# A graph-attention layer and a 32-expert feed-forward on one core: how tokens reach their experts and how the sums come back

## The reference, cut to what matters

```python
N, D, E = 3125, 256, 100000           # nodes, width, edges; 32 experts of hidden width 64
x1 = layernorm(x)
q, k, v = x1 @ wq + bq, x1 @ wk + bk, x1 @ wv + bv
scores = sum(q[dst] * k[src]) * D**-0.5 + edge_weight * we + be
attn = segment_softmax(scores, dst)
y = layer_norm(x1 + segment_sum(v[src] * attn, dst) + x1 @ ws + bs, g1, b1)
y = layer_norm(y + gelu(y @ w_ff1 + b_ff1) @ w_ff2 + b_ff2, g2, b2)
x = x + y
f = layernorm(x)
e = argmax(f @ router_w.T + router_b)   # one expert for each token
h = relu(f @ W1[e] + b1[e])             # W1[e]: 256 x 64
out = x + relu(h @ W2[e] + b2[e])       # W2[e]: 64 x 256
```

## Time and profile before

| | us |
|---|---|
| median of 3 runs | 1901.17 |
| lowest and highest run | 1875.29, 1903.03 |
| span of the profiled execution | 1885.6 |
| PE, DVE, ACT, POOL busy in the span | 1656.9, 1193.9, 965.5, 300.8 |

### The profile page before, as it was taken

One profiled execution on the slowest core, in us unless ns is written; L12 is line 12 of the kernel. 1 busy time (PEld: TensorE's weight loads), 2 busy tenths in 40 slices (PEclk: granted clock), 3 DMA queues, 4 the chain that ended last, 5 costly groups with the idle time before them and its releaser, 6 DMA issues.

```text
span 1885.6 us, 41069 instructions
## 1 busy us (share of the span) xinstructions
PE 1656.9 (88%) x11015; PEld 1378.6 (73%) x11015; DVE 1193.9 (63%) x3327; ACT 965.5 (51%) x2962; POOL 300.8 (16%) x397
## 2 busy tenths in 40 slices
PE   2898999999799999999899999999999789419960
PEld 1796888888688888887688888888888779315640
DVE  3927898988688889898555555555555578701111
ACT  1566888888588888887233333333333345103210
POOL 0022000000000000000111111111110067375435
PEclk9999999999899999999999999999999889656555
DMA  6054333333433333334822222222210100047634
GB/s 159 28 129 115 104 105 104 106 103 105 140 104 104 106 105 103 104 105 112 164 76 77 76 76 76 76 78 75 76 75 37 53 17 0 6 117 214 181 113 121
DMA packets 226999, 180.40 MB, mean 96 GB/s; under 512 B 41884, under 2 KB 218038, under 8 KB 223544
## 3 DMA queue, kind: packets, MB, share of 16 engines
q1 hardware_dynamic: 189327, 112.46, 21.6%
q0 software_dynamic: 21408, 61.20, 9.7%
q10 hardware_dynamic: 16224, 6.27, 1.5%
HBM read 84.94 MB, written 99.11 MB: 98 GB/s over the span
## 4 chain that ended last, share of the span: by engine, by line
PE 78%; DVE 6%; DMA 5%; POOL 4%; issue 3%; SPq 2%; ACT 1%; POOLq 0%; DVEq 0%; ACTq 0%
PE bank L1371 29%; PE bank L1404 15%; PE bank L1392 11%; PE bank L1356 9%; PE bank L1411 3%; PE bank L1486 3%; PE bank L1493 2%; PE bank L1478 2%; PE bank L1444 2%; PE bank L1436 2%; POOL arena L691 2%; POOL xs_dram L669 2%; SPq L458 1%; DMA V<-in_x 1%; DMA arena<-in_x 1%
## 5 line engine op out<-in xcount | busy, mean ns | idle before, releaser
L784 ACT ACTIVATE arena<-bank,tables 128x128 f32<-128x128 f32 x2048 | 585.2, 369 | 144.5 <-PE bank L1356 144.4
L1371 PE MATMUL bank<-arena 128*125 128x128 f32 x4096 | 585.9, 286 | 11.8 <-DVE arena L1055 11.8
L1371 PEld LDWEIGHTS bank<-arena 128*125 128x125 f32 x4096 | 488.4, 188 | 65.1 <-DVE arena L1055 11.9
L1055 DVE TENSOR_TENSOR arena<-iota_row,tables 128x250 f32<-128x250 f32 x1024 | 421.1, 412 | 0.1
L1081 DVE SCALAR_TENSOR_TENSOR arena<-arena,tables,bank 125x128 f32<-125x128 f32 x1023 | 351.9, 344 | 86.5 <-PE bank L1371 37.1
L1404 PE MATMUL bank<-V,arena 125*125 125x256 f32 x1250 | 296.4, 382 | 5.6 <-ACT arena L810 5.6
L810 ACT COPY arena<-bank 125x500 f32<-125x500 f32 (+1 forms) x175 | 90.8, 533 | 379.5 <-PE bank L1411 379.5
L1404 PEld LDWEIGHTS bank<-V,arena 125*125 125x125 f32 x1250 | 223.3, 188 | 38.0 <-ACT arena L810 10.3
L1122 DVE CUSTOM_DVE_ANT_0 arena<-arena 125x3200 f32<-125x3200 f32 x25 | 87.3, 3493 | 222.2 <-ACT arena L793 222.2
L622 POOL COPY gidx<-arow 125x1 uint32 (+1 forms) x25 | 36.4, 1455 | 1182.2 <-DVE wk_sb L1122 856.7
L1356 PE MATMUL bank<-dist_rhs,arena 5*128 5x128 bf16 x2048 | 201.6, 218 | 4.2 <-DVE tables L1039 3.4
(11 more groups left out here) (219 smaller groups left out, 1665.5 us busy)
## 6 DMA issues: line engine op xcount, KB each, us to landing
adj<-arena SPq DMA_DIRECT2D x512, 125.0 KB
xs_dram<-zeros SPq DMA_DIRECT2D x64, 112.0 KB, 3.2
V<-xs_dram SPq DMA_DIRECT2D x56, 128.0 KB, 2.3
ys_dram<-arena SPq DMA_DIRECT2D x56, 128.0 KB, 1.9
w_dram<-in_L_ffn_W SPq DMA_DIRECT2D x2, 2048.0 KB
V<-in_x SPq DMA_DIRECT2D x5, 625.0 KB
q_dram<-arena ACTq DMA_DIRECT2D x25, 125.0 KB, 2.3
wq_sb<-q_dram SPq DMA_DIRECT2D x25, 125.0 KB, 7.8
```

Source lines behind the costliest of these rows:

```text
L784: ins = nc.scalar.activation(Ys[:, q, k, :], bank[2 + s][:, k * LO:(k + 1) * LO], ACT.Relu, scale=nval_tab[:, bass.ds(i, 1)])
L1055: ins = V_.tensor_tensor(Xs[:, s, cols, :], iota_row[:, 0:TILE].unsqueeze(1).to_broadcast([P, SUB, TILE]), code_tab[:, bass.ds(g * GC + k ...
L1371: ins = mm(o, Xs[:, j % STAGES, k, :], Ys[:, j % STAGES, k, :], start=(k % SUB == 0), stop=(k % SUB == SUB - 1))
```

## The change

Blocks are of 64 slots, at most 80 of them, and two blocks form a tile of 128 slots, so there are MJ = 40 tiles. The tokens are stored to `rows_dram` in their own order as the router stage makes them, each row with its `x1` row beside it (2 x 256 elements). After `pos` is known, DVE builds for every tile of nodes a one-hot of the slot within its tile and a one-hot of the tile that holds the node's number; PE multiplies them, and so gets a table: slot to node. POOL then gathers for each tile the rows of its nodes, and after DVE has computed relu plus `x1` row, scatters the 128 rows of the result to the output; slots without a node have a row number out of bounds, and are not written. SP loads each block's expert number into a register and addresses the weights by it. The reload of x has a place of its own and waits for the last scores; each load is split into 112 and 13 rows.

```diff
-MT = (N + NEXP * (P - 1)) // P
-ZROWS = MT * P // (2 * TURNS)
+SLOT = P // 2
+MB = (N + NEXP * (SLOT - 1)) // SLOT
+MJ = MB // 2
+NOWHERE = 8192.0
...
-        x_all = view(NT * D, TILE).rearrange("p (t d) -> p t d", d=D)
+        x_all = tables[0:TILE, 0:NT * D].rearrange("p (t d) -> p t d", d=D)
...
-                   (w_v[:, 0:HID, W2_AT:W2_AT + D], W2), (w_v[:, HID, W2_AT:W2_AT + D], eb2),
-                   (w_v[:, 0:HID, W2_AT + D], eb1), (w_v[:, HID, W2_AT + D:W_ROW], eb2[:, 0:1]),
-                   (w_v[:, XROW:P, W2_AT:W_ROW].rearrange("e r c -> r e c"),
-                    zeros[0:P - XROW, :].unsqueeze(1).to_broadcast([P - XROW, NEXP, D + 1])))
...
+        w_parts = ((w_v[:, 0:HID, 0:D], W2), (w_v[:, HID, 0:D], eb2), (w_v[:, 0:HID, D], eb1), (w_v[:, HID, D:W2_ROW], eb2[:, 0:1]))
...
-                if j % LOADG == 0:
-                    sp.dma_start(xs_dram.ap()[bass.ds((2 * i + j // LOADG) * ZROWS, ZROWS), :],
-                                 zeros[0:ZROWS, 0:D]).then_inc(xs_zeroed, 16)
...
-            sp.wait_ge(x1_ready, NT)
+            sp.wait_ge(s_ready, len(SCH) * NT)
...
-                sp.dma_start(x_all[:, c, :], x_t[:, c, :]).then_inc(nodes_in[i], 16)
...
-                sp.dma_start(xs[:, s, :], node_tile(xs_v, j)).then_inc(xs_in[s], 16)
...
-                sp.dma_start(node_tile(ys_v, j), ys[:, s, :]).then_inc(ys_stored[s], 16)
...
-                sp.dma_start(out_t[:, c, :], x1[:, c, :]).then_inc(out_done, 16)
...
+                for rows_ in (slice(0, EVEN), slice(EVEN, TILE)):
+                    sp.dma_start(x_all[rows_, c, :], x_t[rows_, c, :]).then_inc(nodes_in[i], 16)
+            def put_rows(t, s, u):
+                sp.wait_ge(xf_set, t + 1)
+                sp.dma_start(rows_t[:, bass.ds(t, 1), 0:D].rearrange("p t d -> p (t d)"), node_tile(xf_all, t)).then_inc(rows_stored, 16)
+                sp.dma_start(rows_t[:, bass.ds(t, 1), D:2 * D].rearrange("p t d -> p (t d)"), node_tile(x1, t)).then_inc(rows_stored, 16)
+            each(sp, put_rows)
+            sp.wait_ge(w_made, 16 * len(w_parts))
+            sp.wait_ge(own_set, 1)
+            for j in range(MJ):
+                s = j % ES
+                if j >= ES:
+                    sp.wait_ge(o_ps, j - ES + 1)
+                for h in range(2):
+                    expert = sp.value_load(own_i[2 * j + h:2 * j + h + 1, 0:1], min_val=0, max_val=NEXP - 1)
+                    sp.dma_start(w1s[:, 2 * s + h, :], w1_v[:, bass.ds(expert, 1), :].rearrange("p e c -> p (e c)")
+                                 ).then_inc(w_in[s], 16)
+                    sp.dma_start(w2s[0:XROW, 2 * s + h, :], w2_v[:, bass.ds(expert, 1), :].rearrange("r e c -> r (e c)")
+                                 ).then_inc(w_in[s], 16)
+            for s in range(ES):
+                sp.wait_ge(out_done[s], 16 * (MJ // ES))
...
-            for t in range(NT):
-                nc.gpsimd.indirect_dma_start(xs_dram.ap()[:, :], bass.IndirectOffsetOnAxis(ap=pos_i[:, t:t + 1], axis=0),
-                                             xf_all[:, t, :], None).then_inc(xs_stored, 16)
...
-                nc.gpsimd.tensor_copy(oidx[:, s:s + 1], own_row[:, bass.ds(j, 1)]).then_inc(oidx_set, 1)
-                pool.wait_ge(oidx_set, j + 1)
-                pool.sem_inc(pool_mark, 1)
-                nc.gpsimd.indirect_dma_start(ws_e[:, s, 0:W_ROW], None, w_dram.ap()[:, :],
-                                             bass.IndirectOffsetOnAxis(ap=oidx[:, s:s + 1], axis=0)).then_inc(w_in[s], 16)
...
-                    nc.gpsimd.indirect_dma_start(xf_all[:, t, :], None, ys_dram.ap()[:, :],
-                                                 bass.IndirectOffsetOnAxis(ap=pos_i[:, t:t + 1], axis=0)).then_inc(gath_in[i], 16)
...
+            pool.wait_ge(rows_set, 1)
+            pool.wait_ge(rows_stored, 16 * 2 * NT)
+            for j in range(-AHEAD, MJ):
+                g = j + AHEAD
+                if g < MJ:
+                    if g >= ES:
+                        pool.wait_ge(ys_set, g - ES + 1)
+                    nc.gpsimd.indirect_dma_start(xs[:, g % ES, :], None, rows_dram.ap()[:, :],
+                                                 bass.IndirectOffsetOnAxis(ap=from_row[:, g:g + 1], axis=0)).then_inc(xs_in[g % ES], 16)
+                if j >= 0:
+                    pool.wait_ge(ys_set, j + 1)
+                    nc.gpsimd.indirect_dma_start(out[:, :], bass.IndirectOffsetOnAxis(ap=to_row[:, j:j + 1], axis=0),
+                                                 ys[:, j % ES, :], None, bounds_check=N - 1, oob_is_err=False
+                                                 ).then_inc(out_done[j % ES], 16)
...
-                nc.scalar.activation(hid[0:HID, s, :], bank[j_bank(2, s)][0:HID, 0:P], ACT.Relu,
-                                     bias=w2s[0:HID, s, D:D + 1]).then_inc(hid_set, 1)
+                for b in range(2):
+                    c = slice(b * SLOT, (b + 1) * SLOT)
+                    ins = nc.scalar.activation(hid[0:HID, s, c], bank[j_bank(2, s)][0:HID, c], ACT.Relu,
+                                               bias=w2s[0:HID, 2 * s + b, D:D + 1])
+                ins.then_inc(hid_set, 1)
...
-            V_.tensor_copy(pos_i[:, :], pos[:, :]).then_inc(pos_set, 1)
...
-            V_.tensor_scalar(own_row[:, :], own[:, :], float(P), step_col[:, 0:1], ALU.mult, ALU.add).then_inc(own_set, 1)
...
+            rounded(tile_of[:, :], pos[:, :], 1.0 / P, 0.5 / P - 0.5)
+            od(V_.scalar_tensor_tensor(pos[:, :], tile_of[:, :], -float(P), pos[:, :], ALU.mult, ALU.add))
+            od(V_.tensor_tensor(in_tile, iota_row[0:TILE, 0:MJ].unsqueeze(1).to_broadcast([TILE, NT, MJ]),
+                                tile_of[:, :].unsqueeze(2).to_broadcast([TILE, NT, MJ]), ALU.is_equal))
+            od(V_.tensor_tensor(in_tile, in_tile, node_id[0:TILE, :].unsqueeze(2).to_broadcast([TILE, NT, MJ]), ALU.mult))
+            for i in range(XLOADS):
+                c = slice(i * NT // XLOADS, (i + 1) * NT // XLOADS)
+                shape = [TILE, NT // XLOADS, P]
+                V_.tensor_tensor(in_slot[:, c, :], iota_row[0:TILE, 0:P].unsqueeze(1).to_broadcast(shape),
+                                 pos[:, c].unsqueeze(2).to_broadcast(shape), ALU.is_equal).then_inc(placed, 1)
+            od(V_.tensor_scalar(owner[0:MB, :], tincl[0:MB, :], step_col[0:MB, 0:1], None, ALU.is_le))
+            od(V_.tensor_reduce(own[0:MB, :], owner[0:MB, :], AX, ALU.add))
+            V_.tensor_scalar_min(own_i[0:MB, :], own[0:MB, :], NEXP - 1.0).then_inc(own_set, 1)
+            dve.wait_ge(ids_ps, 1)
+            od(V_.tensor_scalar(slot_id[:, :], bank[4][:, 0:MJ], 0.0, NOWHERE, ALU.is_equal, ALU.mult))
+            od(V_.tensor_scalar(from_row[:, :], bank[4][:, 0:MJ], -1.0, 0.0, ALU.add, ALU.max))
+            V_.scalar_tensor_tensor(to_row[:, :], bank[4][:, 0:MJ], -1.0, slot_id[:, :], ALU.add, ALU.add).then_inc(rows_set, 1)
...
-                V_.tensor_scalar_max(ys[:, s, :], bank[j_bank(4, s)][:, 0:D], 0.0).then_inc(ys_set, 1)
-                V_.tensor_tensor(x1[:, c, :], x1[:, c, :], xf_all[:, c, :], ALU.add).then_inc(o_set, 1)
+                V_.scalar_tensor_tensor(ys[:, s, :], bank[j_bank(4, s)][:, 0:D], 0.0, xs[:, s, D:2 * D], ALU.max,
+                                        ALU.add).then_inc(ys_set, 1)
...
-            pe.wait_ge(pos_set, 1)
+            for i in range(XLOADS):
+                pe.wait_ge(placed, i + 1)
+                for t in range(i * NT // XLOADS, (i + 1) * NT // XLOADS):
+                    ins = mm(bank[4][:, 0:MJ], in_slot[:, t, :], in_tile[:, t, :], start=(t == 0), stop=(t == NT - 1))
+            ins.then_inc(ids_ps, 1)
+            pe.wait_ge(rows_set, 1)
...
-                for k in range(KH):
-                    ins = mm(bank[j_bank(2, s)][0:HID, 0:P], w1s[:, s, k * HID:(k + 1) * HID], xsT[:, s, k * P:(k + 1) * P],
-                             start=(k == 0), stop=(k == KH - 1))
+                for b in range(2):
+                    for k in range(KH):
+                        ins = mm(bank[j_bank(2, s)][0:HID, b * SLOT:(b + 1) * SLOT], w1s[:, 2 * s + b, k * HID:(k + 1) * HID],
+                                 xsT[:, s, k * P + b * SLOT:k * P + (b + 1) * SLOT], start=(k == 0), stop=(k == KH - 1))
...
-                mm(bank[j_bank(4, s)][:, 0:D], hid[0:XROW, s, :], w2s[0:XROW, s, 0:D], start=True, stop=True).then_inc(o_ps, 1)
+                for b in range(2):
+                    c = slice(b * SLOT, (b + 1) * SLOT)
+                    ins = mm(bank[j_bank(4, s)][c, 0:D], hid[0:XROW, s, c], w2s[0:XROW, 2 * s + b, 0:D], start=True, stop=True)
+                ins.then_inc(o_ps, 1)
```

More of the change, by code:

```diff
@@ L53 @@
 SCALE = float(D) ** -0.5
[L54 to L55 removed]
+SLOT = P // 2
+MB = (N + NEXP * (SLOT - 1)) // SLOT
+MJ = MB // 2
+assert MB % 2 == 0
+NOWHERE = 8192.0
 XROW = HID + 1
[L57 removed]
+W2_ROW = D + 1
 SCH = [(c, min(512, ROW - c)) for c in range(0, ROW, 512)]
@@ L119, in gnn_moe @@
         before = sb("before", [P, P])
```

(44 more changed lines are left out.)

59 lines of the change are left out of this document (10 added, 49 removed).

## The result

The changed kernel took **1816.72 us** (median of 4 runs, 1810.27 to 1820.64), beside 1893.41 for the kernel before in the same comparison (4 runs, 1875.29 to 1903.03). The ratio is 0.9637, 95% interval 0.9569 to 0.9705. The forecast was 1808, with a range of 1770 to 1855; it was made against a median before of 1901.17, of three runs, that is a gain of 93 us where this comparison shows 76.7. The profiled execution of after has a span of 1818.9 us, against 1885.6 before: 66.7 less.

The account below looks back on a forecast made before the run. After attention, five bounds in sequence, with PE at 1.2 GHz binding the blocks; -10.1 - 25.2 + 1.6 - 56.6 = -90.3 gives a span of 1795, and set against the median, rounded down by 3, 1808 us, range 1770 to 1855.

Parts of the forecast that it names:

- the likeliest case: Tile stage: PE binds at the low clock, near 3.5 us a tile; the forecast itself, chance 0.46.
- Reload: Start of feed-forward: issuing the reload of x earlier removes PE's hole and slow restart, 10.1 us less (bounds 8.5 and 12).
- Pieces taken out earlier: Before feed-forward: 64 zero stores and two weight copies leave SP; gain 0, bounds 17 below and 5 above.
- From slots to rows: Known slots to PE's first tile: 19.4 us instead of 44.6, 25.2 less (19 to 29).
- Tiles: First tile to last relu: 40 tiles on PE at 1.2 GHz take 138 us, 1.6 more than 136.4.
- So 3.53 binds: Tile stage: PE's 0.63 transposes, 1.70 output and 1.2 hidden layer, 3.53 us a tile, exceed POOL's and SP's needs.
- rival B: Tile stage: POOL binds if PE keeps the high clock or costs less, as with overlapping output halves (2.68); 1791, chance 0.28.
- rival C: Tile stage: register loads bind SP; at 1.7 us a load the run is 1873, under 0.9 nothing shows; chance 0.13.
- C's own formula: Tile stage bound by SP: tiles end at 1641 + 40 s, s being SP's time a tile, with about 10 behind.
- Tail: After the last relu: one scatter, 3.8 us and about 1 of waits, instead of 61.4; 56.6 less (50 if landing is slow).
- Costs set at 0: Feed-forward: SP's 50 row stores cost 0 (2 to 5 us uncovered); tile stage: DVE 0.5 and ACT's short instructions are covered.
- The ring over POOL: Tile stage: gather to relu needs about 6.7 us, two POOL turns and a gather give 2 x 3.5 + 1.3; it fits.

Follow-up runs that it names:

- e4: Changed kernel, but the reload of x waits for the end of attention again, still split into 112 and 13 rows: 1810.6 us.
- e5: Changed kernel, with the reload of x early but each load whole, 125 rows: 1832.93 us.
- e1: Changed kernel, but SP takes each block's expert as a constant, with no register load (wrong experts' weights): 1783.77 us.
- e3: Two-queue kernel (e2), but both output halves go to partitions 0 to 63 and DVE reads them in two instructions: 1799.18 us.
- e2: Changed kernel, but SP loads weights of each tile's first block and ACT the second's (two queues): 1788.46 us, ratio 0.9507.
- e6: Two-queue kernel (e2), with POOL gathering 7 tiles ahead instead of 5: 1819.6 us.
- e12: Changed kernel, with every expert number loaded into a register twice: 1873.72 us.
- e7: Two-queue kernel (e2), with POOL's second early adjacency fetch waiting for 32 further groups: 1808.15 us.
- e10: Two-queue kernel (e2), with the one-hot of slots in bf16 and node numbers split into two bf16 parts: 1806.59 us, ratio 0.9507.
- e9: The two-queue kernel of e2 unchanged, run again on another chip: 1808.22 us, ratio 0.9513.

## Why the prediction was right, and where it was not

**The total** is within the range: 1816.72 for 1808. It looks closer than it is, since the median before had been 7.8 us higher when the forecast was made; in the sum it is -66.7 for -90.3, so 23.6 us are missing, and the likeliest case was not what happened. Step by step:

*Reload: the size right, the reason half right.* The forecast of -10.1 met -9.9. But it took the early place for the cause and left out the split. e4 and e5 show that each does it alone.

*Pieces taken out earlier: cost 0, within bounds of 17 and 5; measured +10.1.* That is a longer adjacency stall (23.28 for 17.52, plus a slow restart). Four kernels that leave the same pieces out and change nothing up to there, e1 to e4, had 17.70, 17.99, 16.12 and 16.45. So the longer stall doesn't come from the pieces; it differs from execution to execution, and its cause is open. The profiled run of after is the longest of its four, 1820.64, and the shortest took 1810.27; without traces of the others, that this is the stall's doing is likely and not shown.

*From slots to rows: right by two errors.* -24.8 for -25.2. The step up to PE's start was 4.2 as forecast. The table took 10.9, not 8.5: the granted clock was 0.50 from its start to its end, the 1.2 GHz level, where the forecast had it rise. The rest of the way was 4.7, not 6.7: the first row was there 3.7 us after POOL began its first gather.

*Tiles: the step that failed.* "So 3.53 binds" rested on 1.70 for the output and on 2.8 for SP. Both were wrong. The output measured 1.05, because its halves overlap (e3: 1.90 without that). The hidden layer, forecast at 1.2, took 1.09, and 0.85 where PE ran without gaps. So PE needed 2.77 in after, and 2.53 without gaps (0.85 + 0.63 + 1.05). That is the condition that rival B named, and its 2.68 was near. The rule behind it, in the Trainium skill, "TensorEngine Tiling (Array Packing)", section "Key Properties", is that different tiles of the array can load and multiply in parallel. The traces agree: 1.05 against 1.90.

What then bound was not POOL, as B had it, but SP, by rival C's mechanism and at a price C did not look for. C asked what a register load would have to cost, above 0.9, and left the rest of the queue at 1.8. Measured are two loads with check at 0.80, 1.6 a tile; four DMA instructions, 1.42; and 0.78 of register work and gaps, where the forecast had 1.0, 1.5 and 0.3. The sum is 3.80, not 2.8, and the tiles took 146.5 where PE's forecast of 138 stood by chance near it. The two errors had opposite signs. C's own formula, a queue that ends at 1641 + 40 s, holds: SP's first load came 10 us later than forecast, at 1651.1, and with s = 3.80 it gives 1803; SP's last weight DMA started at 1804.53. The Trainium skill, "Runtime: NRT & Kernel Launch", section "Instruction fetch mechanics", puts a register load at about 200 ns. The page speaks there of the register loads that the runtime puts in. For the expert numbers, which the kernel reads from on-chip memory, the traces of this case show more: the load alone is 0.50 us (1699.89), and 0.80 with its check.

The low clock itself was forecast rightly: 0.50, with PE busy 77 of 105 us as it had been with 112 of 112. The 5 us that the forecast took off for a first stretch at the high clock did not come: the clock was 0.50 from 1665 to 1685 too.

*Tail: -51.8 for -56.6.* From the start of the last relu to the end it is 9.6 us, not 4.8. The prediction counted one landing of 3.8 and about 1. POOL could start the last scatter only 1.65 us after that relu, behind the one before; and from the end of POOL's queue (1810.34 + 1.64) to 1818.9 it is 6.9, of which a scatter's landing, 2.1 to 3.7 us from its issue in this trace, fills a part. For the rest, the end of the program, the prediction had no row.

*Costs set at 0.* SP's 50 stores of rows, ACT and DVE cost nothing, as forecast: no wait in the chain of after names them. The ring over POOL was "it fits", which holds at SP's pitch of 3.8 and fails below 3 (e1, e2): the prediction counted 6.7 us from gather to relu, and left out the scatter of 1.01 and the waits on both sides of it that make the turn 8.73.

## What to carry to other kernels

Count a queue's whole turn, not its DMAs: with an address from memory, a block of two DMAs held SP for 1.9 us, of which the two DMA instructions were 0.7. When a bound is lifted, ask for the next one before counting the gain: SP's 3.8 hid a ring of about 2.9, which hid PE's 2.53, so that two queues made the tiles 29.7 us shorter and not the 45 that PE's 2.53 a tile alone would have allowed (146.5 less 40 x 2.53). The ring is read from the chains of e1 and e2; e6, which was to try it, is disturbed by another wait. And an edit of two parts that removes a whole wait does not tell which part did it; each may do it alone.

## What the runs showed of the hardware

- Matmuls that write partitions 0 to 63 and 64 to 127 of one bank, with 64 columns of weights each, overlap: four float32 instructions of 256 columns took 1.05 us together and 1.90 when all wrote partitions 0 to 63, both at the 1.2 GHz level.
- A load of a register from on-chip memory on SP takes 0.50 us, its bounds check and gaps another 0.30. A second one right behind it added 0.51 (beside e5) to 0.59 (beside after) a block (e12).
- A load of 125 rows holds SP's queue longer than one of 112 rows and one of 13 together: 30.4 us against 11.4 for five parts of x at the start, 18.6 against 7.5 for the reload. The Trainium skill, "DMA: Bandwidth & Descriptors", "How many engines (k)", ties the number of engines to the divisors of the row count (16 for 112, 13 for 13 and 5 for 125, by its rule); the direction agrees.
- The granted clock stayed at 0.50 both with PE full (e3, 60.0 of 60.0 us from 1700) and with PE busy three quarters of the time (after, through the table and the tiles). In e7 to e10, with PE busy 87 to 89 of 115 us from 1670, it was 0.51 to 0.54.
- The same program has two rhythms, by chip: the two-queue kernel began its adjacency work at 158.5 or at 169.9 us, and its tiles took 117 or 129 us (e2, e9). The slower one goes with waits for "another core or an unknown queue" on ACT and DVE. What makes them is open.
